# A sandwich of two feed-forward blocks around windowed attention: scores computed once and probabilities transposed by DMA

## The chip, the cores and the metric

The kernel runs on one core of a Trainium2 chip. The metric is the time of one execution on the device in microseconds (us). The time of the kernel before is the median of three runs; its profile is of one further execution. TensorE (PE), VectorE (DVE), ScalarE (ACT), GpSimd (POOL) and the queue of SyncE (SP) each take their instructions in the order written and wait for one another by semaphores.

## The reference

The input x is 8 sequences of 512 tokens with 512 features. Three residual blocks follow each other:

```
x = x + 0.5 * ffn(layernorm(x), w_gate_up, w_proj)      # "A"
x = x + attention(layernorm(x), Wq, Wk, Wv, Wo)         # "B"
x = x + 0.5 * ffn(layernorm(x), w_gate_up, w_proj)      # "C"
```

`ffn` quantises both weights to bfloat16 ternary values (per group of 64 elements: scale = mean of the magnitudes, q = round(w/scale) clipped to -1..1, weight = q*scale), computes h = silu(gate)*up with 2048 hidden features, normalises h by its root mean square and projects back. `attention` has 32 heads of 16 features; a query sees itself and the 128 keys before it, so a block of 128 queries needs the keys of its own block and of the block before (of its own alone, if it is the first of its sequence): softmax(q k^T / 4) v, then Wo.

## The kernel before, in words

The 4096 tokens are 32 blocks of 128. A prologue quantises the feed-forward weights in 12 units of 128x2048 (`UNITS`), transposes them on TensorE and keeps them in SBUF. Per unit ScalarE takes magnitudes and signs (`parts`), VectorE sums groups (`scales`) and compares, adds and multiplies (`quantise`); GpSimd forms 'scale minus magnitude' (`differ`) and multiplies by the sign in five of the units (`give_sign`), with an all-reduce of the maxima after the eighth. Between units the first block's gate and up products run. VectorE then takes the largest magnitude of each attention weight (`largest`), GpSimd reduces it over the partitions, and the attention weights are scaled and split in steps 2 to 10.

Then comes a software pipeline. Every engine and the SP queue walk through `range(STEPS)`, and each step runs the pieces whose offset fits: `block_at(step, offset)` is the block b with step = offset + 8b, `group_at(step, offset)` is the pair (block, group) for pieces that run once per step. So a new block enters every 8 steps, and each of its stages has an offset (`UP_A`, `Q_AT`, `SCORES`, `PV`, `UP_C`, ...). A's feed-forward chunks of block b run in steps 8b to 8b+3, C's in steps 8b+36 to 8b+39. From step 36 to step 251 every step therefore holds one feed-forward chunk of 512 hidden features, of A (step mod 8 = 0 to 3) or of C (4 to 7), and one group of 4 heads of some block in each attention stage. Before and after these steps only part of them holds a chunk. STEPS is 8*31 + 42 = 290. In a step:

- TensorE: `scores` (four matmuls 128x256, queries in the partitions), the gate product, the up product, `scores_t` (eight matmuls 128x128, keys in the partitions), `down` of the chunk of the step before, `prob_v`, and in steps mod 8 = 0, 1, 3, 7 a projection of 12 matmuls 128x512 (Q, K, V, Wo).
- VectorE: square means, `masked_max` (row maxima of the group, with the mask added), low halves of q, k, v, of the layer norms' splits, residual additions, `normalise_o` in even steps, the low half of o, then `gated`, `hidden`, the low half of the probabilities, the low half of the hidden values (`h_lo`), and last the layer norms' statistics and `xhat`.
- ScalarE: high halves of q, k, v, xh and oh, `tanh_half` (of the gate product), the high half of the probabilities, two Relu that scale `scores_t` into `prob`, `h_hi`, the square, and one Exp over 128x1024 (or half of that in a sequence's first block).
- GpSimd: small powers, the sum of the squares, and two `affine_select` that mask `prob`.
- SP: one transposing DMA for each of q, k, xh (A, B, C) and oh in a block, plus one more of q after `max_rows` has written the negative row maxima of the whole block into spare rows of q. The transposed scores thus arrive with the maximum subtracted, which is why they start a block later (`SCORES_T` = 20) than `scores` (12).

Keys come in two halves of 128 (the block before and the block itself); in the first block of a sequence only the second exists, and the operands of the scores, maxima and probabilities are half as wide. Values of 32 bits are carried as a high and a low half of 16 bits.

The transposed scores stand in a ring of three banks, `ps_s` (`score_bank`). Two waits of the kernel before on ScalarE matter for the order of a step: the tanh waits for the gate product alone, and `oh` in steps mod 8 = 6 waits for the last normalisation of its block:

```
    s, b, c = ffn_at(step)
    if s and not (s == "A" and b == 0):
        tanh_half(s, b, c, step)
    ...
    act.wait_ge(p_st, 16 * b + 2 * g + o + 1)
```

## Time and profile before

| | |
|---|---|
| median of 3 runs | 2278.78 us (2277.72 to 2279.49) |
| profiled execution | 2278.95 us, of which the span of instructions is 2277.2 us |
| mean granted TensorE clock | 0.961 of 2.4 GHz |
| busy over the span: PE | 2063.2 us (91%) |
| DVE | 1784.5 us (78%) |
| ACT | 1401.9 us (62%) |
| POOL | 768.5 us (34%) |
| DMA queue of SP | 117.47 MB, 25.7% of 16 engines' span |

Busy time is an average over a prologue of about 150 us, a ramp, a steady part and a drain. A start time in the timeline, counted from the span's start, dates a step; the difference of two starts on one engine is what an instruction takes there, waits included, while a mean duration also holds latency in which the next instruction may already run. The idle time ahead of a group of instructions is listed with the engine and the instruction that ended it.

### The profile page before, as it was taken

The numbers are of one execution on the slowest core, as the hardware profiler recorded it, in microseconds if no ns is written. First come the engines' busy times: TensorE is split into PE (matmuls) and PEld (weight loads), VectorE is DVE, ScalarE is ACT, GpSimd is POOL, SyncE is SP. The second block draws the span as 40 slices with busy tenths as digits, with TensorE's granted clock in tenths as the row PEclk, the third lists the DMA queues.
The fourth block names the chain that finished last, engine by engine and source line by source line (L and its number), as shares of the span: only waits on it lengthen the run. The fifth ranks groups of instructions, "written<-read, shape, count | busy, mean of one in ns | idle before, by whom it ended". The sixth has DMA issues, their size and how long they took to land. (4 is left out here: it accounts for less than half of the span.)

```text
span 2277.2 us, 64890 instructions
## 1 busy us (share of the span) xinstructions
PE 2063.2 (91%) x26752; PEld 1496.5 (66%) x26752; DVE 1784.5 (78%) x4393; ACT 1401.9 (62%) x2073; POOL 768.5 (34%) x963
## 2 busy tenths in 40 slices
PE   1327789999999999999999999999999999999877
PEld 1315557777777777777777767777777777776556
DVE  8965678787887788877887878878878888887764
ACT  5523357665676566765767566765666566666672
POOL 4431123332333333333333333333333233333332
PEclk9668889999999999999999999999999999999989
DMA  4221222222332222222322222332223222223210
GB/s 161 74 83 29 52 47 53 53 48 57 57 50 44 46 48 57 57 53 48 57 58 54 39 46 49 57 57 52 48 57 57 57 36 46 49 52 48 43 34 20
DMA packets 351269, 121.62 MB, mean 53 GB/s; under 512 B 336128, under 2 KB 336128, under 8 KB 350464
## 3 DMA queue, kind: packets, MB, share of 16 engines
q1 hardware_dynamic: 350976, 117.47, 25.7%
q8 instruction: 213, 3.49, 0.6%
q14 instruction: 80, 0.66, 0.1%
HBM read 25.17 MB, written 8.39 MB: 15 GB/s over the span
## 5 line engine op out<-in xcount | busy, mean ns | idle before, releaser
L778 DVE CUSTOM_DVE_ANT_0 masked<-ps_s,mask 128x256 f32<-128x256 f32 (+1 forms) x1024 | 338.4, 386 | 199.3 <-PE ps_s L983 199.1
L622 ACT ACTIVATE prob<-ps_s,neg_exp_scale 128x512 f32<-128x512 f32 (+1 forms) x512 | 295.9, 629 | 123.2 <-PE ps_s L997 123.2
L504 POOL TENSOR_TENSOR acc_A<-acc_A,sq 128x512 f32<-128x512 f32 x96 | 125.7, 1310 | 568.2 <-ACT sq L639 568.0
L536 ACT ACTIVATE hid<-ps_g 128x512 f32<-128x512 f32 x256 | 151.8, 593 | 259.9 <-PE ps_g L950 259.8
L752 DVE TENSOR_TENSOR pt<-prob,pt 128x1024 f16<-128x1024 f32 (+1 forms) x256 | 276.8, 1081 | 6.9 <-ACT pt L614 6.9
L1007 PE MATMUL ps_y<-wp_t,h_hi 128*128 128x512 bf16 x1024 | 267.2, 384 | 14.9 <-ACT h_hi L532 14.9
L504 POOL TENSOR_TENSOR acc_C<-acc_C,sq 128x512 f32<-128x512 f32 x96 | 134.0, 1395 | 434.8 <-ACT sq L639 434.8
L645 ACT ACTIVATE prob<-prob,prob_bias 128x1024 f32<-128x1024 f32 (+1 forms) x256 | 265.0, 1035 | 0.6
L1007 PE MATMUL ps_y<-wp_t,h_lo 128*128 128x512 bf16 x1024 | 264.6, 381 | 0.0
L950 PE MATMUL ps_g<-xt_C,wgu_t 128*128 128x128 f16 x4096 | 255.0, 221 | 7.4 <-DMA xt_C<-xh 6.8
L950 PE MATMUL ps_g<-xt_A,wgu_t 128*128 128x128 f16 x4096 | 260.5, 224 | 1.3 <-DMA xt_A<-xh 1.3
L614 ACT ACTIVATE pt<-prob 128x1024 f16<-128x1024 f32 (+1 forms) x256 | 241.5, 943 | 24.8 <-POOL prob L514 24.8
L950 PEld LDWEIGHTS ps_g<-xt_A,wgu_t 128*128 128x128 bf16 x4096 | 239.1, 100 | 23.9 <-issue 18.7
L950 PEld LDWEIGHTS ps_g<-xt_C,wgu_t 128*128 128x128 bf16 x4096 | 233.6, 99 | 29.8 <-issue 18.5
L767 DVE SCALAR_TENSOR_TENSOR hid<-ps_u,h_scale_u,hid 128x512 f32<-128x512 f32 x252 | 189.2, 751 | 80.7 <-PE ps_u L950 51.8
L950 PE MATMUL ps_u<-xt_A,wgu_t 128*128 128x128 f16 x4096 | 250.6, 219 | 0.0
L950 PE MATMUL ps_u<-xt_C,wgu_t 128*128 128x128 f16 x4096 | 249.6, 219 | 0.0
L950 PEld LDWEIGHTS ps_u<-xt_A,wgu_t 128*128 128x128 bf16 x4096 | 235.3, 98 | 0.0
L512 POOL TENSOR_SCALAR_AFFINE_SELECT prob<-prob 128x512 f32<-128x512 f32 x192 | 130.0, 677 | 310.3 <-ACT prob L645 310.3
L950 PEld LDWEIGHTS ps_u<-xt_C,wgu_t 128*128 128x128 bf16 x4096 | 234.1, 98 | 0.0
L752 DVE TENSOR_TENSOR h_lo<-hid,h_hi 128x512 f16<-128x512 f32 x256 | 176.4, 689 | 46.0 <-ACT h_hi L532 44.1
L532 ACT ACTIVATE h_hi<-hid 128x512 f16<-128x512 f32 x256 | 161.1, 629 | 70.7 <-DVE hid L767 52.5
(152 smaller groups left out, 3311.3 us busy)
## 6 DMA issues: line engine op xcount, KB each, us to landing
stream<-in_L_attn_x_dram SPq DMA_DIRECT2D x32, 256.0 KB, 3.7
out_dram<-stream SPq DMA_DIRECT2D x32, 256.0 KB, 2.5
stream<-in_L_ffn_w_gate_up_dram SPq DMA_DIRECT2D x4, 1024.0 KB, 5.2
prob<-in_L_ffn_w_gate_up_dram SPq DMA_DIRECT2D x4, 1024.0 KB, 5.6
stream<-in_L_ffn_w_proj_dram SPq DMA_DIRECT2D x2, 1024.0 KB, 4.9
prob<-in_L_ffn_w_proj_dram SPq DMA_DIRECT2D x2, 1024.0 KB, 4.8
stream<-in_L_attn_Wq_dram SPq DMA_DIRECT2D x1, 1024.0 KB, 5.4
prob<-in_L_attn_Wk_dram SPq DMA_DIRECT2D x1, 1024.0 KB, 7.6
```

The costliest lines, as they stand in the source:

```text
L504: pool.tensor_tensor(out=acc[s][:, :], in0=acc[s][:, :], in1=sq[:, step % 2, :], op=ALU.add).then_inc(g_acc[s], 1)
L512: pool.affine_select(out=p4[:, :, 0, :], in_=p4[:, :, 0, :], compare_op=ALU.is_ge, fill=0.0, base=0, pattern=[[0, 4], [-1, P]], channel_mu ...
L532: act.activation(dst, src, ACT.Copy, scale=scale).then_inc(done, 1)
L536: act.activation(hid[:, step % 2, :], ps_g[:, :], ACT.Tanh, scale=0.5 * 2.0 ** -XS_LOG2).then_inc(a_tanh[s], 1)
L614: act.activation(halves(pt[:, 0, g % 2, :, :], b), halves(prob[:, g % 2, :, :], b), ACT.Copy).then_inc(a_ph, 1)
L622: act.activation(halves(prob[:, g % 2, 4 * o:4 * o + 4, :], b), halves(score_bank(step, 2 + o).rearrange("p (t q) -> p t q", q=P), b), ACT ...
L645: act.activation(p, p, ACT.Exp, bias=prob_bias[:, 0:1], scale=-1.0).then_inc(a_exp, 1)
L752: dve.tensor_tensor(out=dst, in0=src, in1=hi, op=ALU.subtract).then_inc(done, 1)
L767: dve.scalar_tensor_tensor(out=dst, in0=ps_u[:, :], scalar=scale, in1=hid[:, step % 2, :], op0=ALU.mult, op1=ALU.mult).then_inc(d_h[s], 1)
L778: m = dve.tensor_tensor_reduce(masked[:, g % 2, 2 * pair + o, first:2 * P], score_bank(step, o)[:, pair * 2 * P + first:(pair + 1) * 2 * P ...
L950: t = pe.matmul(bank[:, j * P:(j + 1) * P], wgu_t[:, k, at:at + P], xt[s][:, part, k, :], start=(k == 0 and part == 0), stop=(k == KD - 1 ...
L1007: t = pe.matmul(ps_y[:, :], part[:, (step - 1) % 3, j * P:(j + 1) * P], wp_t[:, 4 * c + j, :], start=(c == 0 and j == 0 and part is h_hi), ...
```

## The change

Scores are computed once, with the queries in the partitions, and the probabilities are formed there. The masked scores that `masked_max` writes stay in `masked`. ScalarE turns the group's four row maxima into biases (an Identity operation of 128x4) and runs four Exp in place, one for each head, in the step of the scores and ahead of the tanh. One step later ScalarE writes the high half and VectorE the low half of the probabilities, now ahead of the other work of the step, and SP transposes both halves with one DMA into `pt`; `prob_v` follows in the step after. `scores_t`, its two Relu, the 128x1024 Exp, `max_rows`, its transpose of q and GpSimd's masks go. All attention stages behind the scores and the whole of C move 8 steps forward, so that a block passes through 34 steps instead of 42 (STEPS = 282). The ring of score banks becomes two fixed banks, and the sums of squares get a bank of their own (`ps_q`).

In the prologue ScalarE widens the group scales to 128x2048 (`spread`, into the space of k4), VectorE subtracts the magnitudes itself and multiplies by the sign in all 12 units, and ScalarE's order becomes signs, store, magnitudes of the next unit, spread. The maxima of the attention weights move into steps 0 and 1, behind the hidden values. The number that stands for a masked key is -2^100 for -3e38.

```diff
-    M_AT = SCORES + 7
-    SCORES_T = 20
-    PROB = SCORES_T + 1
-    PV = SCORES_T + 2
+    PROB = SCORES + 1
+    PV = SCORES + 2
     NORM = PV + 1
-    SPLIT_O, WO_AT = NORM + 7, 31
-    LN_C, XHAT_C, SPLIT_C = 32, 33, 34
-    UP_C, SQ_C, ADD_C = 36, 40, 41
+    SPLIT_O, WO_AT = NORM + 7, 23
+    LN_C, XHAT_C, SPLIT_C = 24, 25, 26
+    UP_C, SQ_C, ADD_C = 28, 32, 33
...
@@ SyncE @@
-                b = block_at(step, M_AT)
-                if b is not None:
-                    sp.wait_ge(d_m, b + 1)
-                    sp.wait_ge(p_s, 16 * b + 16)
-                    transpose(qt[:, b % QRING, :, :], q4[:, b % 2, :, :, :].rearrange("p a b c -> p (a b c)"), t_qm)
+                b, g = group_at(step, PROB)
+                if b is not None:
+                    sp.wait_ge(d_pl, 8 * b + g + 1)
+                    need(sp, p_pv, 8 * b + g - 1)
+                    first = first_half(b)
+                    transpose(pt[:, g % 2, first:2, :, :, :].rearrange("p a b c d -> p (a b c) d"),
+                              prob[:, g % 2, first:2, :, :, :].rearrange("p a b c d -> p (a b c d)"), t_p[g % 2])
...
@@ GpSimd @@
-            for n in range(NTU):
-                differ(n)
-                if n % 2 == 0 and n > 0:
-                    give_sign(n - 1)
...
-                b, g = group_at(step, SCORES_T)
-                if b is not None:
-                    p4 = prob[:, g % 2, :, :].rearrange("p (j h) q -> p j h q", h=2)
-                    pool.wait_ge(a_exp, 8 * b + g + 1)
-...
@@ ScalarE, prologue @@
+            def spread(n):
+                act.wait_ge(w_grp, n + 1)
+                need(act, w_dif, n)
+                act.activation(w_wide.rearrange("p (g k) -> p g k", g=G64),
+                               grp_scale[:, n % 2, :].unsqueeze(2).to_broadcast([P, G64, 64]),
+                               ACT.Copy).then_inc(w_spread, 1)
...
@@ ScalarE, in a step, behind the copies of q, k, v @@
+                b, g = group_at(step, PROB)
+                if b is not None:
+                    act.wait_ge(a_exp, 8 * b + g + 1)
+                    need(act, t_p[g % 2], 16 * (4 * b + g // 2))
+                    act.activation(prob_part(prob[:, g % 2, :, 0, :, :], b), prob_f32(b, g), ACT.Copy).then_inc(a_ph, 1)
@@ ScalarE, in a step, behind xh and oh @@
+                b, g = group_at(step, SCORES)
+                if b is not None:
+                    act.wait_ge(d_mx, 16 * b + 2 * g + 2)
+                    need(act, a_exp, 8 * (b - 1) + g + 1)
+                    act.activation(exp_bias[:, 4 * g:4 * g + 4], row_max[:, 4 * g:4 * g + 4], ACT.Identity,
+                                   bias=prob_bias[:, 0:1], scale=neg_exp_scale[:, 0:1]).then_inc(a_bias, 1)
+                    act.wait_ge(a_bias, 8 * b + g + 1)
+                    for h in range(4):
+                        p = masked[:, g % 2, h, P * first_half(b):2 * P]
+                        t = act.activation(p, p, ACT.Exp, bias=exp_bias[:, 4 * g + h:4 * g + h + 1],
+                                           scale=exp_scale[:, 0:1])
+                    t.then_inc(a_exp, 1)
+
                 s, b, c = ffn_at(step)
                 if s and not (s == "A" and b == 0):
                     tanh_half(s, b, c, step)
...
@@ VectorE, quantise @@
+                dve.wait_ge(w_spread, n + 1)
+                need(dve, w_q[n % 2], n // 2)
+                dve.tensor_tensor(out=diff, in0=w_wide, in1=w, op=ALU.subtract).then_inc(w_dif, 1)
...
@@ VectorE, in a step, behind the low half of v @@
+                b, g = group_at(step, PROB)
+                if b is not None:
+                    take_lo(prob_part(prob[:, g % 2, :, 1, :, :], b), prob_f32(b, g),
+                            prob_part(prob[:, g % 2, :, 0, :, :], b), a_ph, 8 * b + g + 1, d_pl)
...
@@ TensorE @@
-                b, g = group_at(step, SCORES_T)
-                if b is not None:
-                    need(pe, a_neg, 2 * groups_by(step - 1, SCORES_T))
-                    need(pe, d_mx, 2 * groups_by(step, SCORES) - (group_at(step, SCORES)[0] is not None))
-                    if g == 0:
-                        pe.wait_ge(t_qm, 16 * (b + 1))
-                    scores_t(b, g, step)
...
                 b, g = group_at(step, PV)
                 if b is not None:
-                    pe.wait_ge(d_pl, 8 * b + g + 1)
+                    pe.wait_ge(t_p[g % 2], 16 * (4 * b + g // 2 + 1))
```

## Rows read from the trace of the kernel before

**Rows 1.** Stretches of time: length, then busy us (instructions) of each engine, clock, DMA.
```profile
800.00:1600.00 800.00, 791.10 (x10464) 572.15 (x10461) 648.26 (x1695) 523.12 (x800) 277.83 (x367) 1.00 0.28 52
...
2105.00:2132.00 27.00, 19.98 (x188) 9.98 (x189) 18.41 (x63) 16.39 (x20) 8.37 (x14) 0.81 0.43 79
```
**Rows 2.** Timeline of TensorE in two steps: start, us, operation.
```profile
1355.86 0.39 PE L983 MATMUL ps_s<-kt,qt 48*128 48x256 f16 x4
...
1365.02 0.39 PE L983 MATMUL ps_s<-kt,qt 48*128 48x256 f16 x4
...
1369.02 0.40 PE L997 MATMUL ps_s<-qt,kt 64*128 64x128 f16 x8
...
1371.57 0.39 PE L983 MATMUL ps_s<-kt,qt 48*128 48x256 f16 x4
```
**Rows 3.** Timeline of ScalarE: the tanh of steps 24, 36 and 252.
```profile
285.87 0.60 ACT L536 ACTIVATE hid<-ps_g 128x512 f32<-128x512 f32 x1 [2.93 <-PE ps_g L950]
...
371.51 0.60 ACT L536 ACTIVATE hid<-ps_g 128x512 f32<-128x512 f32 x1 [1.56 <-PE ps_g L950]
...
2077.61 0.60 ACT L536 ACTIVATE hid<-ps_g 128x512 f32<-128x512 f32 x1 [1.56 <-PE ps_g L950]
```
**Rows 4.** Groups of ScalarE by shape, 800 to 1600 us: busy us, mean ns | idle before.
```profile
L645 ACT ACTIVATE prob<-prob,prob_bias 128x1024 f32<-128x1024 f32 x76 | 86.9, 1143 | 0.0
L614 ACT ACTIVATE pt<-prob 128x1024 f16<-128x1024 f32 x75 | 78.8, 1050 | 1.3 <-POOL prob L514 1.3
...
L645 ACT ACTIVATE prob<-prob,prob_bias 128x512 f32<-128x512 f32 x26 | 18.5, 710 | 0.0
```
**Rows 5.** Timeline of all engines in the drain, where the feed-forward chain runs almost alone.
```profile
2229.41 0.68 DVE L761 SCALAR_TENSOR_TENSOR hid<-hid,ps_g 128x512 f32<-128x512 f32 x1
...
2230.29 0.75 DVE L767 SCALAR_TENSOR_TENSOR hid<-ps_u,h_scale_u,hid 128x512 f32<-128x512 f32 x1 [0.20 <-PE ps_u L950]
...
2231.13 0.63 ACT L532 ACTIVATE h_hi<-hid 128x512 f16<-128x512 f32 x1 [1.88 <-DVE hid L767]
...
2231.80 0.69 DVE L752 TENSOR_TENSOR h_lo<-hid,h_hi 128x512 f16<-128x512 f32 x1 [0.76 <-ACT h_hi L532]
...
2233.65 0.60 ACT L536 ACTIVATE hid<-ps_g 128x512 f32<-128x512 f32 x1 [1.37 <-PE ps_g L950]
```
**Rows 6.** Timeline of VectorE in the steady part.
```profile
1228.05 0.69 DVE L738 BATCH_NORM_STATS2 st_C<-stream 128x6 f32<-128x512 f32 x1
...
1229.06 0.21 DVE L809 TENSOR_SCALAR sq_mean_C<-ps_o,rms_eps 128x1 f32<-128x1 f32 x1
...
1236.71 0.69 DVE L752 TENSOR_TENSOR h_lo<-hid,h_hi 128x512 f16<-128x512 f32 x1 [0.22 <-ACT h_hi L532]
1237.32 1.50 DVE L747 TENSOR_SCALAR xhat<-stream,mean_var_C,rstd_C 128x512 f32<-128x512 f32 x1
...
1242.07 0.42 DVE L798 TENSOR_REDUCE o_sum<-ps_o 128x128 f32<-128x256 f32 x1
...
1242.90 0.68 DVE L761 SCALAR_TENSOR_TENSOR hid<-hid,ps_g 128x512 f32<-128x512 f32 x1
...
1255.63 0.42 DVE L778 CUSTOM_DVE_ANT_0 masked<-ps_s,mask 128x256 f32<-128x256 f32 x1 [1.71 <-PE ps_s L983]
...
1257.01 0.08 DVE L778 DVE_READ_ACCUMULATOR2_ANT row_max<- 128x1 f32 x1
```
**Rows 7.** Groups of VectorE in the prologue, 0 to 178 us.
```profile
L674 DVE TENSOR_TENSOR kt<-kt,q 128x2048 bf16<-128x2048 bf16 x12 | 41.8, 3480 | 6.9 <-POOL q L448 6.9
...
L676 DVE TENSOR_TENSOR q<-kt,q 128x2048 bf16<-128x2048 bf16 x12 | 21.3, 1773 | 0.4
...
L661 DVE TENSOR_SCALAR grp_scale<-grp_sum 128x32 bf16<-128x32 f32 x12 | 11.1, 921 | 0.4
...
L683 DVE TENSOR_TENSOR pt<-q,qt 128x2048 bf16<-128x2048 bf16 x7 | 8.6, 1225 | 0.2
```
**Rows 8.** DMA issues: times, median us from issue to landing.
```profile
qt<-q SPq DMA_TRANSPOSE x64, 4.4
```

More of the change, by code:

```diff
@@ L48, in macaron @@
     V_LOG2 = 19
-    M_LOG2 = 15
     RING = 8
@@ L639, in step_of @@
                     act.activation(squares, hid[:, step % 2, :], ACT.Square).then_inc(a_sq[s], 1)
-                b, g = group_at(step, SCORES_T)
-                if b is not None:
-                    act.wait_ge(a_neg, 16 * b + 2 * g + 2)
-                    p = halves(prob[:, g % 2, :, :], b)
-                    act.activation(p, p, ACT.Exp, bias=prob_bias[:, 0:1], scale=-1.0).then_inc(a_exp, 1)
             for step in range(STEPS):
@@ L768, in hidden, with masked_max @@
                                          op0=ALU.mult, op1=ALU.mult).then_inc(d_h[s], 1)
[L770 to L772 removed]
+            def masked_max(b, g):
+                need(dve, d_pl, 8 * b + g - 1)
+                need(dve, a_bias, 8 * (b - 1) + g + 1)
                 first = 0 if b % BPS else P
@@ L905, in step_of @@
                         hidden(s, bf, c, hid[:, step % 2, :], step, h_scale_u[:, 0:1])
-                b, g = group_at(step, PROB)
-                if b is not None:
-                    take_lo(halves(pt[:, 1, g % 2, :, :], b), halves(prob[:, g % 2, :, :], b),
-                            halves(pt[:, 0, g % 2, :, :], b), a_ph, 8 * b + g + 1, d_pl)
+                if step in (0, 1):
+                    for m in ((Q, K), (V, O))[step]:
+                        largest(m)
                 if s:
@@ L975, in project, with scores @@
                 t.then_inc(done, 1)
-            def scores(b, g, step):
+            def scores(b, g):
                 place = b % BPS
@@ L982, in scores @@
                         rows = slice(64 * o, 64 * o + 3 * DK)
-                        t = pe.matmul(score_bank(step, o)[:, pair * 2 * P + (0 if place else P):(pair + 1) * 2 * P],
+                        at = o * CH + pair * 2 * P
+                        t = pe.matmul(ps_s[:, at + P * first_half(b):at + 2 * P],
                                       qt[rows, b % QRING, 2 * g + pair, :],
@@ L988, in scores @@
                             t.then_inc(p_s, 1)
-            def scores_t(b, g, step):
-                place = b % BPS
-                for pair in range(2):
-                    for half in ((0, 1) if place else (1,)):
-                        for o in range(2):
-                            at = pair * 2 * P + half * P
-                            rows = slice(64 * o, 64 * o + 64)
-                            t = pe.matmul(score_bank(step, 2 + o)[:, at:at + P],
-                                          kt[rows, 2 * g + pair, place - 1 + half, :],
-                                          qt[rows, b % QRING, 2 * g + pair, :], start=True, stop=True)
-                            if pair and half:
-                                t.then_inc(p_st, 1)
             def down(s, b, c, step):
@@ L1018, in prob_v @@
                         for n, (half, part) in enumerate(products):
-                            t = pe.matmul(ps_o[:, at:at + VW], pt[:, part, g % 2, (o * 2 + pair) * 2 + half, :],
+                            t = pe.matmul(ps_o[:, at:at + VW], pt[:, g % 2, half, part, 2 * pair + o, :],
                                           v[:, place - 1 + half, hd, 0:VW], start=(n == 0), stop=(n == len(products) - 1))
@@ L1051, in step_of @@
                     need(pe, d_mx, 2 * groups_by(step - 1, SCORES))
-                    need(pe, a_neg, 2 * groups_by(step - 1, SCORES_T) - 1)
                     if g == 0:
@@ L1055, in step_of @@
                         pe.wait_ge(t_k, 16 * (b + 1))
-                    scores(b, g, step)
+                    scores(b, g)
                 s, b, c = ffn_at(step)
@@ L1104, in step_of @@
                         need(pe, d_on, 4 * b + g // 2)
-                    for sq_s, offset in (("A", SQ_A), ("C", SQ_C)):
-                        bs = block_at(step - 1, offset)
-                        if bs is not None:
-                            pe.wait_ge(d_sqm[sq_s], bs + 1)
                     prob_v(b, g)
```

155 lines of the change are left out of this document (58 added, 97 removed).

## The prediction

> **What bounds the kernel now.** I read the stretches first. Between 800 and 1600 us TensorE is busy for 791 of 800 us at full clock, VectorE for 648, ScalarE for 523 and GpSimd for 278, and the DMA engines for 0.28 of the time [rows 1]. So in the steady part TensorE sets the pace, but VectorE is only a fifth behind it. Then TensorE's timeline: a step without a projection lasts 6.55 us (scores at 1365.02, the next scores at 1371.57), one with a projection 9.16 us (1355.86 to 1365.02), and the transposed scores span 0.40 us of each [rows 2]. Four of the eight steps of a block carry a projection (step mod 8 = 0, 1, 3, 7). Then ScalarE's tanh of the first chunk of a phase, which dates the steps: step 24 at 285.87, step 36 (where C's FFN starts) at 371.51, step 252 at 2077.61 [rows 3]. So 216 full steps, 27 blocks, take 1706.1 us: 63.2 us a block.
>
> **What leaves TensorE.** The transposed scores go: about 0.33 us a step once the overlap of the last matmul is taken off the 0.40 [rows 2], 2.6 us a block. TensorE's own work was 0.989 of 63.2 us [rows 1], 62.5 us, and falls to 59.9. Call it 60.8 with the short gaps between steps. By that alone the change would be a clear gain.
>
> **What is added to the chain between VectorE and ScalarE.** Here I chose another reading than "the busiest engine". Before, the tanh of step s waited only for TensorE. Now ScalarE's order in a step is: bias, four Exp, then tanh. The bias waits for the row maxima of the same step, and on VectorE these stand behind h_lo of step s-1. h_lo needs h_hi, that needs hidden, that needs gated, and that needs tanh of s-1. So there is a loop of exactly one step that TensorE takes no part in. Its links, from rows:
> The four masked maxima: 1.38 us to the last read, 0.08 for it, 1.46 (1255.63 to 1257.01) [rows 6]. Handing over to ScalarE 0.10, as from hidden to h_hi below. The bias operation (128x4): ScalarE's 128x512 and 128x1024 exponentials differ by 433 ns, 0.85 ns an element; the 1024 copy without a pointer takes 93 ns less than the exponential with one (1050 against 1143) [rows 4]. So the fixed part without a pointer is about 0.2 us, with two pointers (scale and bias) 0.385, and 0.03 for the wait on itself. Bounds: 0.2 and 0.5. The new Exp (128x256, two pointers): 710 less 216 is 494, plus 93 is 587 ns; starts follow each other about 0.10 us closer than durations, so 0.485, and four are 1.94 us. Bounds: 1.58 if the second pointer is free, 2.35 if nothing overlaps. Tanh 0.60 (2233.65) and 0.03 to gated, as from the end of h_hi to h_lo. From gated to hidden 0.88 (2229.41 to 2230.29), to h_hi 0.84, to h_lo 0.67 [rows 5]. To the next operation of VectorE 0.61 (1236.71 to 1237.32) [rows 6], and 0.1 for the wait for the scores. Sum: 7.65 us for every step, against 6.2 us of TensorE's work in a step without a projection and 8.8 in one with it.
>
> What stands in the loop beside that depends on the step. Between the maxima and gated VectorE has about 3.1 us for other work (the low half of the probabilities, the same operation as before, somewhat over a microsecond; a normalisation 0.83, 1242.07 to 1242.90 [rows 6]; one or two operations of 0.6 to 0.7), which covers it. Behind h_lo there is no cover. Statistics cost 1.0 (1228.05 to 1229.06) in steps 0, 3 and 5; xhat of A 0.5 in step 4; xhat of B and C 1.4 in steps 6 and 1, since their row shows 1.50 us at the moment GpSimd adds the squares (1237.32) [rows 6], which the change leaves there. In step 6 ScalarE's copy of o_norm waits for maxima, probabilities, split and normalisation in turn and stands ahead of the bias: 3.0 us more, where before it stood ahead of a tanh that did not wait for maxima. The eight steps from step 0: 8.75, 8.95, 7.65, 8.6, 8.1, 8.6, 12.0, 7.65, together 70.4 us. TensorE would need 60.8, and its projections fall in steps where the loop has caught up, so they add nothing. In the first block of a sequence (one in four) the operands are half as wide: by the same slopes the maxima take 0.93 and the exponentials 1.50 (estimates), so 6.7 for a step; there TensorE's projection steps lead again in steps 1 and 3, and I work out 63.7. With 21 blocks of the one and 7 of the other a block costs 68.7 us, 5.5 more than now.
>
> Beside the sum stands a rule of the Trainium skill, "VectorE: DVE Perf Modes", section "The TRN2 errata": operations that read SBUF pay a fixed latency per instruction, many small tiles pay it each time, and ScalarE's is given as 224 cycles plus one per element. That speaks against four 256-wide exponentials in place of a 1024-wide one. An estimate by that page is 0.40 us for each, 1.6 for four, 0.34 less per step than my rows give; the total would be about 2320 us. No row shows a 256-wide exponential.
>
> **The transposes.** Eight transposes of the probabilities are added per block and the one of the row maxima goes. One of this size lands in 4.4 us [rows 8]. The DMA share of 0.28 [rows 1] is 17.7 us a block for three of the 512 KB size, four of half the size and two plain 256 KB ones. With 0.7 us for a plain one, a large one fills all engines for 3.2 us. After: ten large ones, 39 us of 68.7. The low half is ready 2.5 to 3.1 us behind the start of the maxima, the product with v comes some 13 us behind them, so there are about 5 us to spare even behind another transpose. On SP the new one stands ahead of those of xt_B, xt_C, xt_A and ot; each of these has a step or more. I take nothing for it. If that cover went, SP's next waits would hold xt and with it the gate product.
>
> **GpSimd's masks and the max rows** leave engines that don't bind: nothing. With them the wait for rms_inv goes too.
>
> **The weights phase.** VectorE sets it. The comparison takes 3.48 us in the mean where GpSimd runs, with 6.9 us of waiting besides; the addition 1.77; the scale 0.92 against a quiet 0.18, an estimate from its smallest neighbours; a product without a neighbour 1.225 [rows 7]. Without GpSimd: (3.48-1.22)x12 + (1.77-1.22)x12 + (0.92-0.2)x12 + 6.9 = 49 us less. Added on VectorE: 12 subtractions and 5 products of 1.25, 21 us. Net 28 us. ScalarE's widened copy (1.8 us by the same width) fits: its unit is some 7.3 us against VectorE's 8.8. The maxima of the attention weights now lie between other work, some 4 us more. Together 32 us; bounds 20 and 36.
>
> **Fewer steps.** Full steps go from 216 to 224, 28 blocks. To the first full step: the eight steps that go are the 85.6 us from step 24 to 36 less four full steps (31.6), 54 [rows 3]. So 371.5, less 32, less 54, plus 5 for the loop in the early attention steps: 291. Behind the last full step before lie 38 steps in 2277.2-2077.6 = 199.6 us, 5.25 each; 30 remain, 158, and 10 for the loop: 168. Sum: 291 + 28 x 68.7 + 168 = 2383 us of span. The profiled execution was 1.75 us longer than its span (2278.95) and agrees with the median, 2278.78, within 0.2. So **2385 us**, 4.7% slower. The same line gives the break-even: 64.9 us a block.
>
> **The rivals.**
> *TensorE stays the bound* (the other side). If bias, exponentials and tail were shorter, so that a step of the loop averaged under 7.6 us and not 8.6, each block would cost 60.8: 291 + 1702 + 168 + 2 = 2163 us. For it: ScalarE and VectorE both have idle time. Against: the order of the instructions, in which that idle time is waiting. It beats the old time once a block is under 64.9. Chance 0.08.
> *The second pointer and the short operations cost nothing*: 0.54 less a step, mid blocks 66.1, first ones 62.3, so 65.2 a block and 2286 us. Chance 0.05, 0.03 of it within the bound of no change, 0.02 below.
> *TensorE's clock falls.* It now idles some 8 us a block. Where it was busy for 20 of 27 us the granted clock was 0.81 [rows 1], a mix of 1.2 and 2.4 GHz. At that clock its 60.8 us become 75 and bind: 2561 us. Against: it stays near 0.9 busy. Chance 0.09, most of it for a part of this price.
> *The transposes bind.* If ten large ones took 6.1 and four small ones 4 us one after another, a block would be 78 us and the time 2645. Chance 0.04.
>
> **Range.** From 2300 (block 65.7: the low bounds of Exp and bias with the xhat stalls kept) to 2420 (block 70.0 or a few us more in the ends: no overlap of the Exps). It leaves out TensorE's case, most of the clock's and the transposes'. Within 0.2% is about what a measurement of this kernel can tell from no change. Slower 0.74+0.09+0.04 = 0.87, same 0.03, faster 0.08+0.02 = 0.10.
>
> **What would show it.** Right: in the steady part TensorE falls to about 0.88 busy and waits ahead of the gate product for VectorE's gated; ScalarE's first Exp or bias waits for row_max; the step mod 8 = 6 is the longest at 12 us; the product with v never waits for DMA; steady blocks of 68 to 70 us with a short one in four; weights done 30 us earlier. Wrong: if TensorE still runs at 0.98, if the Exps overlap more than 0.10 us, if xhat no longer takes 1.50, or if waits for pt appear.

## The result and the profile after

The changed kernel takes 2438.66 us (median of four runs, 2437.78 to 2438.86) against 2278.25 before (2277.25 to 2279.49): ratio 1.070 [1.0685, 1.0722]. The forecast was 2385 us with a range of 2300 to 2420. The direction was right, and so was the loop that was to set the pace; the time lies 54 us above the forecast and 19 above the range. The profiled execution has a span of 2436.8 us and a mean granted clock of 0.928 (0.961 before).

The stretches first, the same 800 us as in [rows 1]:

```profile
800.00:1600.00 800.00, 713.01 (x8816) 526.94 (x8813) 586.72 (x1504) 493.02 (x899) 156.28 (x171) 0.95 0.51 92
```

All four engines are less busy than before, TensorE at 0.89 for 0.99: none of them is the bound by its sum. The DMA share has gone from 0.28 to 0.51. Then the waits of the same stretch (who waited for whom: us in total, times, longest):

```profile
ACT h_hi L504 <- DVE hid L754: 159.7, 90, 2.1
DVE hid L748 <- ACT hid L508: 98.1, 89, 2.2
...
ACT exp_bias L602 <- DVE row_max L765: 54.8, 56, 2.1
...
ACT oh L504 <- DVE o_norm L780: 44.9, 12, 4.2
PE ps_g L924 <- DVE hid L748: 40.1, 12, 3.6
...
PE ps_y L969 <- DVE stream L792: 26.3, 20, 2.4
PE ps_o L981 <- DVE o_norm L780: 20.6, 21, 1.8
```

ScalarE and VectorE wait for each other in turn, which is what a loop through both looks like, and TensorE waits for what VectorE hands it. No wait of TensorE for a transposed `pt` is among them. One turn of the loop stands in the timeline of a step mod 8 = 3 (start, us, operation):

```profile
1201.45 0.42 DVE L765 CUSTOM_DVE_ANT_0 masked<-ps_s,mask 128x256 f32<-128x256 f32 x1
...
1202.95 0.39 ACT L602 ACTIVATE exp_bias<-row_max,prob_bias,neg_exp_scale 128x4 f32<-128x4 f32 x1 [0.67 <-DVE row_max L765]
...
1203.37 2.07 ACT L607 ACTIVATE masked<-masked,exp_bias,exp_scale 128x256 f32<-128x256 f32 x4
...
1205.35 0.57 ACT L508 ACTIVATE hid<-ps_g 128x512 f32<-128x512 f32 x1
...
1205.96 0.69 DVE L748 SCALAR_TENSOR_TENSOR hid<-hid,ps_g 128x512 f32<-128x512 f32 x1 [1.91 <-ACT hid L508]
...
1206.86 0.75 DVE L754 SCALAR_TENSOR_TENSOR hid<-ps_u,h_scale_u,hid 128x512 f32<-128x512 f32 x1 [0.21 <-DVE hid L748]
...
1207.70 0.63 ACT L504 ACTIVATE h_hi<-hid 128x512 f16<-128x512 f32 x1 [1.78 <-DVE hid L754]
...
1208.37 0.69 DVE L739 TENSOR_TENSOR h_lo<-hid,h_hi 128x512 f16<-128x512 f32 x1 [0.76 <-ACT h_hi L504]
...
1208.97 0.69 DVE L725 BATCH_NORM_STATS2 st_A<-stream 128x6 f32<-128x512 f32 x1
...
1210.06 0.42 DVE L765 CUSTOM_DVE_ANT_0 masked<-ps_s,mask 128x256 f32<-128x256 f32 x1
```

From the first maximum to the first operation behind h_lo it is 7.52 us (1201.45 to 1208.97), then 1.09 of statistics, and the next step begins. The forecast's sum was 7.65, of which 0.1 was for a wait for the scores that does not occur here. The new operations came out as sized, by shape in 800 to 1600 us:

```profile
L607 ACT ACTIVATE masked<-masked,exp_bias,exp_scale 128x256 f32<-128x256 f32 x280 | 145.2, 589 | 2.3
...
L602 ACT ACTIVATE exp_bias<-row_max,prob_bias,neg_exp_scale 128x4 f32<-128x4 f32 x91 | 35.1, 385 | 54.9 <-DVE row_max L765 54.8
```

An Exp takes 589 ns (587 forecast, from the slopes of [rows 4]), the bias 385 (385). Four Exp span 2.07 us, and tanh starts 1.98 behind the first (1.94 forecast).

By the tanh of steps 28 and 252 (303.15 and 2260.80) the span divides into 303.2 + 28 x 69.92 + 176.0. The forecast was 291 + 28 x 68.7 + 168. So 34 us of the miss lie in the steady part, 12 in the ramp, 8 in the drain.

### The profile page after: what moved, and what is told of

Same layout as the page of the kernel before. It is cut to its first block and busy times, and to the rows that moved or that the text cites. A ratio compares the mean times of both kernels' runs of the same rounds, so it can differ in the third digit from the quotient of the medians.

```text
span 2436.8 us, 61174 instructions
## 1 busy us (share of the span) xinstructions
PE 2049.2 (84%) x24960; PEld 1513.8 (62%) x24960; DVE 1761.1 (72%) x4347; ACT 1482.2 (61%) x2597; POOL 439.2 (18%) x497
## 5 line engine op out<-in xcount | busy, mean ns | idle before, releaser
L607 ACT ACTIVATE masked<-masked,exp_bias,exp_scale 128x256 f32<-128x256 f32 (+1 forms) x1024 | 503.7, 562 | 8.6
L924 PE MATMUL ps_g<-xt_C,wgu_t 128*128 128x128 f16 x4096 | 303.0, 243 | 108.3 <-DVE hid L748 101.3
L748 DVE SCALAR_TENSOR_TENSOR hid<-hid,ps_g 128x512 f32<-128x512 f32 x256 | 176.0, 688 | 277.5 <-ACT hid L508 277.0
L924 PEld LDWEIGHTS ps_g<-xt_C,wgu_t 128*128 128x128 bf16 x4096 | 278.5, 110 | 134.5 <-DVE hid L748 115.1
L739 DVE TENSOR_TENSOR prob<-masked,prob 128x1024 f16<-128x1024 f32 (+1 forms) x256 | 283.2, 1106 | 5.4 <-ACT prob L586 5.4
L924 PE MATMUL ps_u<-xt_C,wgu_t 128*128 128x128 f16 x4096 | 280.6, 233 | 0.0
L924 PEld LDWEIGHTS ps_u<-xt_C,wgu_t 128*128 128x128 bf16 x4096 | 266.7, 106 | 0.0
L586 ACT ACTIVATE prob<-masked 128x1024 f16<-128x1024 f32 (+1 forms) x256 | 240.0, 937 | 0.4
L981 PEld LDWEIGHTS ps_o<-v,pt 128*128 128x128 f16 x3584 | 122.9, 96 | 167.3 <-issue 103.1
L981 PE MATMUL ps_o<-v,pt 128*128 128x33 f16 x3584 | 129.9, 178 | 93.9 <-DVE o_norm L780 76.1
```

Of the source, the lines that this page charges most:

```text
L586: act.activation(prob_part(prob[:, g % 2, :, 0, :, :], b), prob_f32(b, g), ACT.Copy).then_inc(a_ph, 1)
L607: t = act.activation(p, p, ACT.Exp, bias=exp_bias[:, 4 * g + h:4 * g + h + 1], scale=exp_scale[:, 0:1])
L739: dve.tensor_tensor(out=dst, in0=src, in1=hi, op=ALU.subtract).then_inc(done, 1)
L748: dve.scalar_tensor_tensor(out=hid[:, step % 2, :], in0=hid[:, step % 2, :], scalar=1.0, in1=ps_g[:, :], op0=ALU.add, op1=ALU.mult).then_i ...
L924: t = pe.matmul(bank[:, j * P:(j + 1) * P], wgu_t[:, k, at:at + P], xt[s][:, part, k, :], start=(k == 0 and part == 0), stop=(k == KD - 1 ...
L981: t = pe.matmul(ps_o[:, at:at + VW], pt[:, g % 2, half, part, 2 * pair + o, :], v[:, place - 1 + half, hd, 0:VW], start=(n == 0), stop=(n ...
```

## The experiments

All are edits of the changed kernel unless they say "the kernel before". "A block" is a quarter of the time between ScalarE's copies of q of blocks 13 and 17, which holds one first block of a sequence and three others; it is 63.2 us before and 70.0 us after.

| run | us | ratio to before | a block |
|---|---|---|---|
| after | 2438.7 | 1.070 | 70.0 |
| e1 tanh first | 2217.3 | 0.973 | 62.4 |
| e2 Exp last | 2412.1 | 1.059 | 68.9 |
| e3 one Exp | 2312.0 | 1.015 | 65.8 |
| e4 before, new weights phase | 2249.2 | 0.987 | 63.2 |
| e5 oh late | 2321.5 | 1.019 | 65.8 |
| e6 half transposes | 2434.8 | 1.069 | 70.0 |
| e7 tanh first, oh late | 2202.3 | 0.967 | 61.9 |
| e8 = e7, additions early | 2165.2 | 0.950 | 60.7 |
| e9 norms early | 2346.8 | 1.030 | 66.9 |
| e10 an extra operation | 2520.5 | 1.106 | 72.6 |
| e11 before, the same extra | 2300.5 | 1.010 | 63.8 |
| e12 = e8, norms early | 2165.0 | 0.950 | 61.5 |
| e13 short projections | 2375.4 | 1.043 | 68.1 |

The intervals of the ratios are 0.0014 to 0.0019 to either side.

### e1: the tanh ahead of bias and Exp

```diff
@@ ScalarE, in a step @@
+                s, b, c = ffn_at(step)
+                if s and not (s == "A" and b == 0):
+                    tanh_half(s, b, c, step)
                 b, g = group_at(step, SCORES)
                 if b is not None:
...
-                s, b, c = ffn_at(step)
-                if s and not (s == "A" and b == 0):
-                    tanh_half(s, b, c, step)
```

> The changed kernel with ScalarE's tanh issued ahead of the bias and the four Exp of the same step, nothing else. Theory (the loop maxima - bias - Exp - tanh - gated - hidden - h_hi - h_lo sets the step): tanh, gated and hidden leave the loop, what is left of it is 1.46 + 0.10 + 0.42 + 1.94 + 0.67 + 0.71 = 5.3 us, below TensorE's 6.2, so TensorE sets most steps again; only the step mod 8 = 6, where the copy of o_norm waits for VectorE, stays at some 10 us. A block of 63 to 65 us for 69.9, 2250 to 2290 us in all. Rival one (the transposes through DMA or the waits of the product with v and of ps_y bind): the time stays within 10 us of 2438. Rival two (VectorE's and ScalarE's work itself, not its order, is too much): 2400 us or more.

2217.3 us, ratio 0.973 [0.9713, 0.9746]: 221 us from one moved instruction, and more than was expected. It leaves no room for either rival: the same transposes, the same work on each engine, another order. ScalarE in a step mod 8 = 4 of this kernel:

```profile
1235.56 0.60 ACT L508 ACTIVATE hid<-ps_g 128x512 f32<-128x512 f32 x1 [1.04 <-PE ps_g L924]
1236.05 0.38 ACT L606 ACTIVATE exp_bias<-row_max,prob_bias,neg_exp_scale 128x4 f32<-128x4 f32 x1
1236.46 2.07 ACT L611 ACTIVATE masked<-masked,exp_bias,exp_scale 128x256 f32<-128x256 f32 x4
1238.95 0.63 ACT L504 ACTIVATE h_hi<-hid 128x512 f16<-128x512 f32 x1 [0.42 <-DVE hid L754]
```

Between tanh and h_hi ScalarE has to wait for gated and hidden in any case. The bias and the four Exp now fill that gap, and 0.42 us of waiting is left of the 1.78 in the changed kernel. The tanh waits for TensorE again.

### e2: bias and Exp at the end of ScalarE's step

```diff
@@ ScalarE, in a step: the block of bias and Exp moved @@
                     act.activation(squares, hid[:, step % 2, :], ACT.Square).then_inc(a_sq[s], 1)
+                b, g = group_at(step, SCORES)
+                if b is not None:
+                    act.wait_ge(d_mx, 16 * b + 2 * g + 2)
...
```

> The changed kernel with bias and Exp moved to the end of ScalarE's step, behind h_hi and the square. Theory of the loop: nothing of the FFN chain waits for the maxima of its own step any more; what is left is the maxima to Exp to the high half of the probabilities of the next step, with slack. TensorE binds at 60.8 us a block but for step 6: 61 to 63.5 us a block, 2190 to 2255 us. If TensorE's clock falls or the transposes bind instead, 2330 us or more, because the probabilities now come later; waits of TensorE for pt would show.

2412.1 us: the time is 157 us above the expected range, and its reason fails with it. It falls among the times of the rival (2330 or more), but not for the rival's reasons: between 800 and 1600 us TensorE never waits for pt, and its mean clock is 0.96 for 0.95. ScalarE from one h_hi to the next:

```profile
1195.33 0.63 ACT L504 ACTIVATE h_hi<-hid 128x512 f16<-128x512 f32 x1 [2.43 <-DVE hid L754]
1195.87 0.61 ACT L615 ACTIVATE sq<-hid 128x512 f32<-128x512 f32 x1
1196.39 0.37 ACT L621 ACTIVATE exp_bias<-row_max,prob_bias,neg_exp_scale 128x4 f32<-128x4 f32 x1
1196.79 2.08 ACT L626 ACTIVATE masked<-masked,exp_bias,exp_scale 128x256 f32<-128x256 f32 x4
...
1199.25 1.04 ACT L586 ACTIVATE prob<-masked 128x1024 f16<-128x1024 f32 x1
1200.20 0.58 ACT L508 ACTIVATE hid<-ps_g 128x512 f32<-128x512 f32 x1
1204.04 0.63 ACT L504 ACTIVATE h_hi<-hid 128x512 f16<-128x512 f32 x1 [3.26 <-DVE hid L754]
```

VectorE in the same turn:

```profile
1200.33 1.23 DVE L739 TENSOR_TENSOR prob<-masked,prob 128x1024 f16<-128x1024 f32 x1 [0.25 <-ACT prob L586]
...
1202.30 0.68 DVE L748 SCALAR_TENSOR_TENSOR hid<-hid,ps_g 128x512 f32<-128x512 f32 x1
```

Nothing waits for the maxima here, and still a step takes 8.7 us (1195.33 to 1204.04). Steps are cyclic: behind h_hi of one step is ahead of the tanh of the next, so the Exp still stand between h_hi and tanh. The edit also adds a wait that the changed kernel does not have. The high half of the probabilities now comes right behind the Exp that feed it, and VectorE's low half, which stands ahead of gated, waits for it: 69.0 us in 66 waits between 800 and 1600 us, none in the changed kernel. Gated starts at 1202.30, 1.5 us behind the end of the tanh, and ScalarE idles 3.26 us until hidden. The 27 us of gain are the sum of both effects, so e2 does not price the chain through the maxima alone.

That two chains run side by side in the changed kernel, VectorE's through the maxima and ScalarE's own of square, high half, bias, Exp and tanh, is seen in its own trace. In the turn of 7.52 us shown above the bias waited 0.67 us for the maxima, so ScalarE's own sequence would have taken some 6.9 (an estimate from these two numbers). Between 800 and 1600 us 56 of the 91 bias operations waited for a maximum, 35 did not. e1 takes the Exp out of both chains.

### e3: one Exp for four

```diff
-                    for h in range(4):
-                        p = masked[:, g % 2, h, P * first_half(b):2 * P]
-                        t = act.activation(p, p, ACT.Exp, bias=exp_bias[:, 4 * g + h:4 * g + h + 1],
-                                           scale=exp_scale[:, 0:1])
+                    p = masked[:, g % 2, :, P * first_half(b):2 * P]
+                    t = act.activation(p, p, ACT.Exp, bias=prob_bias[:, 0:1], scale=tiny[:, 0:1])
```

> The changed kernel, but the group's Exp is one instruction over 128x1024 with a constant bias and a constant small scale, both by pointer, so every probability is about the same number: the maxima are taken and the bias operation is issued but not used. Order and all waits as in the changed kernel. It sizes the term of the four Exp. Theory of the loop: 1.94 us becomes about 1.05, 0.9 us less in every step that the loop sets, some 6 us a block and 165 to 185 us in all with the ramp: 2255 to 2275 us. Rival (DMA or TensorE waits bind): under 30 us less.

2312.0 us, 127 us less; 165 to 185 were expected. The row of the new Exp, against four that span 2.07 us:

```profile
L608 ACT ACTIVATE masked<-masked,prob_bias,tiny 128x1024 f32<-128x1024 f32 x74 | 91.8, 1241 | 2.5
```

It saves 0.83 us a step, 6.6 a block if every step were set by the loop; 4.2 came back. In a middle block the steps mod 8 = 3, 5 and 6 are 0.84 us shorter, steps 2 and 4 by 0.44 and 0.57, and steps 0 and 1 keep their 8.94 and 9.31 us: something else sets them (e13).

### e4: the new weights phase in the kernel before

The edits of the prologue alone (`spread`, `magnitudes`, `signs`, `quantise`, the maxima in steps 0 and 1) in the kernel before; its steps stay.

> The kernel before with the new weights phase alone (widened scales from ScalarE, VectorE subtracts and signs, the maxima of the attention weights in steps 0 and 1); its steps are untouched. Theory: VectorE's units fall from some 11 us to 8.7, and the whole is 30 us earlier, 2248 us. If the gain is lost in the ramp (attention weights, which come in fixed steps), 2260 us or more.

2249.2 us, 29 us less, ratio 0.987 [0.9859, 0.9888]. The forecast had 32 (28 of it for the units, bounds 20 and 36). Q of the first block is copied 28.9 us earlier than before and the block is the same 63.2, so the gain reaches the end whole. The rows of VectorE in the changed kernel's first 150 us show how well a clean neighbour's duration carries over [rows 7]:

```profile
L662 DVE TENSOR_TENSOR q<-kt,q 128x2048 bf16<-128x2048 bf16 x12 | 14.7, 1225 | 0.4
L660 DVE TENSOR_TENSOR kt<-kt,q 128x2048 bf16<-128x2048 bf16 x12 | 14.7, 1225 | 0.4
```

### e5: the copy of o_norm behind the tanh

```diff
@@ ScalarE: behind tanh_half instead of ahead of bias and Exp @@
+                b = block_at(step, SPLIT_O)
+                if b is not None:
+                    need(act, t_o, 16 * b)
+                    copy(oh[:, 0, :], o_norm[:, :], d_on, 4 * b + 4, a_oh)
@@ VectorE: the low half behind hidden instead of ahead of gated @@
+                b = block_at(step, SPLIT_O)
+                if b is not None:
+                    take_lo(oh[:, 1, :], o_norm[:, :], oh[:, 0, :], a_oh, b + 1, d_ol)
```

> The changed kernel with one piece moved: in the step mod 8 = 6 ScalarE's copy of o_norm comes behind the tanh and not ahead of the bias and the Exp, and VectorE's low half of o behind hidden. Theory of the loop: the 12.1 us step falls to about 8, 4 us a block; TensorE then idles less ahead of step 7, its clock there stays up, and it is less late for the scores of steps 7 to 2, up to 1 us more. 65 to 66 us a block for 69.9, 2300 to 2335 us. If TensorE's clock drop in step 7 were what counts by itself, the gain would be 6 us a block, under 2275 us; if something else holds step 6, under 30 us of gain.

2321.5 us, 117 us less, within the range of the loop theory. The changed kernel's long step, mod 8 = 6, in its timeline:

```profile
1230.90 0.63 ACT L504 ACTIVATE oh<-o_norm 128x512 f16<-128x512 f32 x1 [3.88 <-DVE o_norm L780]
...
1235.18 3.60 PE L924 MATMUL ps_g<-xt_C,wgu_t 128*128 128x128 f16 x32 [3.35 <-DVE hid L748]
...
1238.87 0.41 DVE L765 CUSTOM_DVE_ANT_0 masked<-ps_s,mask 128x256 f32<-128x256 f32 x1
```

The step lasts 12.10 us (from 1226.77), 12.0 forecast, and 8.96 in e5. TensorE idles 3.35 us behind it, and then the gate product takes 3.60 us for the usual 1.96. The stretches show why (the clock is the third figure from the right):

```profile
1235.20:1238.20 3.00, 3.00 (x29) 3.00 (x30) 2.12 (x3) 2.03 (x3) 0.81 (x1) 0.50 0.19 36
...
1242.00:1246.00 4.00, 4.00 (x35) 1.96 (x32) 1.74 (x4) 2.23 (x5) 0.00 (x0) 1.00 0.92 175
```

At 0.50, the lower of the two levels (1.2 of 2.4 GHz), TensorE loses 1.6 us there and another 1.1 in the up product (3.07 us for 1.95), and is late into the next steps. In e5 the mean clock between 800 and 1600 us is 0.99 for 0.95, and the steps mod 8 = 7 and 0 are 0.48 and 0.28 us shorter. So of 4.2 us a block 3.1 are the long step itself and under one comes from the steps behind it.

### e6: half of the transposed bytes

```diff
-                    first = first_half(b)
+                    first = 1
                     transpose(pt[:, g % 2, first:2, :, :, :].rearrange("p a b c d -> p (a b c) d"),
```

> The changed kernel, but each DMA of the probabilities transposes only the keys of the block itself (256 KB for 512 KB); in place of the other half the product with v reads ones. Order and waits stay. Theory (transposes are hidden): under 10 us from 2438. If they cost time, through the product with v, the queue of SP or the DMA engines: 30 us or more faster.

2434.8 us, 4 less, and the same 70.0 a block, while the DMA share between 800 and 1600 us falls from 0.51 to 0.37: in the steady part of the changed kernel the transposes are free.

### e7 and e8: the order that beats both kernels

e7 joins the edits of e1 and e5, but its copy of o_norm stands ahead of bias and Exp (in e5 it stands behind them). e8 moves three pieces of VectorE as well:

```diff
@@ VectorE, in a step: ahead of the low half of the probabilities @@
+                b = block_at(step, ADD_A)
+                if b is not None:
+                    add_ffn("A", b, d_x1)
+                b = block_at(step, ADD_C)
+                if b is not None:
+                    add_ffn("C", b, d_x3)
+                b, g = group_at(step, NORM)
+                if b is not None and g % 2:
+                    normalise_o(b, g // 2)
                 b, g = group_at(step, PROB)
                 if b is not None:
                     take_lo(prob_part(prob[:, g % 2, :, 1, :, :], b), prob_f32(b, g),
```

> Tanh ahead of bias and Exp (as in the first run) and the copy of o_norm behind both tanh and ahead of the bias, the low half of o behind hidden. There TensorE idles some 3 us a block, and the step mod 8 = 6 still lasts 11.2 us. Theory: about 1.5 us a block comes back, 2165 to 2195 us. If TensorE binds fully already: no change from 2217.

> As the run before, and on VectorE the two residual additions of the FFN and the normalisation of o are moved ahead of the low half of the probabilities. TensorE's waits for ps_y (18 us in 800) and ps_o (8 in 800) should go, which is 2 us a block at the most; the probabilities come 0.8 us later in half of the steps, hidden. 2130 to 2185 us, at least 10 us below the run before. Rival: the low half comes too late for the next scores' buffers or for the transposes, and TensorE's waits move to pt: no gain.

e7: 2202.3 us, 15 less than e1; 22 to 52 were expected. e8: 2165.2 us, ratio 0.950 [0.9488, 0.9516], 37 less again. TensorE's waits ahead of its products into ps_y and ps_o, which the forecast had not named, are 18.3 and 7.8 us between 800 and 1600 us in e1, still 13.9 and 14.9 in e7, and gone in e8. Its steady part:

```profile
800.00:1600.00 800.00, 781.88 (x10182) 575.09 (x10179) 668.80 (x1743) 572.58 (x1042) 166.09 (x197) 1.00 0.61 106
```

TensorE is 0.98 busy at full clock, with 60.7 us a block. That is the 60.8 the forecast had for a TensorE-bound block, and 2165 us is the 2163 of its first rival. So the change, with another order on two engines, is 5% faster than the kernel before; 1.3% of it is the weights phase (e4). A small wait for a transpose does appear in this faster kernel: TensorE waits 5.9 us in these 800 for ot. What the early additions would give the kernel before was not tested; its TensorE was busy for 791 of 800 us already [rows 1].

### e9: statistics and xhat ahead of gated

The pieces `LN_B` to `XHAT_A` of VectorE's step move from behind h_lo to the place before `gated`.

> The changed kernel with one piece of VectorE's step moved: the statistics and the xhat of the layer norms stand ahead of gated, where the prediction says that 3.1 us lie free, and not behind h_lo, where it says that there is no cover. Theory of the prediction (the loop runs through the maxima): of the 6.3 us a block that stood behind h_lo 3 to 5 go: 65 to 67 us a block, 2290 to 2350 us. Rival (ScalarE's own sequence h_hi, square, high half of the probabilities, bias, Exp, tanh is nearly as long, and the maxima are mostly in time): under 1.5 us a block, 2395 us or more.

2346.8 us, 3.1 us a block less, within the range expected by the forecast's theory and far from its rival. Part of it has another source. Between 800 and 1600 us, the changed kernel and then e9:

```profile
L734 DVE TENSOR_SCALAR xhat<-stream,mean_var_B,rstd_B 128x512 f32<-128x512 f32 x12 | 18.1, 1506 | 0.0
L734 DVE TENSOR_SCALAR xhat<-stream,mean_var_C,rstd_C 128x512 f32<-128x512 f32 x11 | 16.6, 1505 | 0.0
```

```profile
L734 DVE TENSOR_SCALAR xhat<-stream,mean_var_B,rstd_B 128x512 f32<-128x512 f32 x12 | 6.5, 541 | 0.0
L734 DVE TENSOR_SCALAR xhat<-stream,mean_var_C,rstd_C 128x512 f32<-128x512 f32 x12 | 6.5, 539 | 0.0
```

The same instruction takes 0.54 us once it no longer starts as GpSimd adds the squares. Two of them make up to 1.9 us a block. e9 does not separate that from the place in the loop. The step mod 8 = 1 keeps its 9.31 us even without the long xhat.

### e10 and e11: an operation that nobody reads

```diff
+                if s:
+                    dve.tensor_reduce(extra[:, :], mask[:, :].unsqueeze(1).to_broadcast([P, 2, 2 * P]), AX.X, ALU.max)
                 b = block_at(step, LN_B)
```

> The changed kernel with an operation added on VectorE behind h_lo in every step with a chunk: a maximum over a constant, 128x512, about 0.6 us, that nobody reads. Theory of the prediction: all of it enters the loop in the steps that the maxima set, 4 to 4.7 us a block, 2550 to 2575 us. Rival (ScalarE's own sequence): it is absorbed for the most part, under 2480 us.

> The same added operation in the kernel before. TensorE binds there and VectorE idles some 12 us of 63 a block: 2278 to 2295 us. If VectorE's chain is close behind TensorE there too, 2310 us or more.

The row of the changed kernel's variant, 680 ns, about 0.6 from start to start:

```profile
L892 DVE TENSOR_REDUCE extra<-mask 128x2 f32<-128x512 f32 x87 | 59.1, 679 | 0.0
```

e10 costs 82 us, between the two expectations. By steps mod 8 = 0 to 7 of a middle block the lengths went from 8.94, 9.31, 8.00, 8.61, 8.11, 8.60, 12.10, 7.98 to 9.24, 9.30, 8.60, 9.21, 8.71, 9.19, 12.11, 8.11. In steps 2 to 5 the whole 0.6 arrives: VectorE's chain through h_lo and the maxima sets these steps alone. In steps 1 and 6 nothing arrives, and that is no proof of slack: there the xhat of C and of B stands behind the added operation, starts 0.6 us further into GpSimd's addition and takes 0.916 us for 1.505 (all 22 of them between 800 and 1600 us), which gives the 0.6 back. The forecast of e10 had not seen this. Steps 0 and 7 take up part of it. In the kernel before the same operation costs 22 us, a little above the range expected: TensorE's bound absorbs most of it.

### e12: e9's edit on e8

> The eighth run (tanh ahead, o late, additions early; 2165 us) with the statistics and xhat ahead of gated. TensorE binds at 60.7 us a block there, so the steady part has nothing to give: 2150 to 2175 us. If gated comes later than TensorE can bear, 2180 us or more.

2165.0 us, the same as e8 within 0.2. Where TensorE is the bound, what the loop loses is worth nothing. (The block reads 61.5 because one of its four took 3 us more; the next four average 60.8.)

### e13: projections of 4 matmuls

```diff
-                    for n, (part, w) in enumerate(((0, wat_hi), (0, wat_lo), (1, wat_hi))):
-                        t = pe.matmul(ps_m[:, :], tokens[:, part, k, :], w[m][:, k, :], start=(k == 0 and n == 0),
-                                      stop=(k == KD - 1 and n == 2))
+                    t = pe.matmul(ps_m[:, :], tokens[:, 0, k, :], wat_hi[m][:, k, :], start=(k == 0),
+                                  stop=(k == KD - 1))
```

> The changed kernel, but each projection (Q, K, V, Wo) keeps the product of the two high halves alone, 4 matmuls for 12; the other two products are left out, so q, k, v and the output lack their low parts. It tests the step 'the projections fall in steps where the loop has caught up, so add nothing'. A step was 8.94, 9.31, 8.00 and 7.98 us long at step mod 8 = 0, 1, 2, 7 where the prediction had 8.75, 8.95, 7.65 and 7.65; step 1 stayed at 9.30 in four other variants. Theory now (in these four steps the projection and ScalarE's copy of it enter the loop, and in the ramp and the drain, where TensorE runs at the low clock, a projection of 5 us does): 0.7 to 1.3 us a block and 5 to 20 us in the ends, 2385 to 2415 us. If the prediction's step holds and the excess is from elsewhere: 2428 us or more.

2375.4 us, 63 less, more than was expected, and nowhere near "hidden". In middle blocks the steps mod 8 = 0, 1, 2 and 7 now last 8.65, 8.94 to 9.20, 7.55 or 8.00, and 7.50 us, for 8.75, 8.95, 7.65 and 7.65 in the prediction: without two thirds of each projection they come close to what the loop alone was to give. VectorE's waits for the scores ahead of the maxima fall from 12.2 us (33 times) between 800 and 1600 us to 0.2 (once), and ScalarE's waits for the projections of q are gone. The clock is no rival here, since its mean between 800 and 1600 us is 0.94, no higher than before the edit (0.95). The block loses 1.8 us, the ramp up to step 28 10.5, the drain 5. The changed kernel's own timeline shows the place, the turn from step 1 to step 2:

```profile
1192.57 0.38 PE L947 MATMUL ps_m<-wk_hi,xt_B 128*128 128x512 f16 x1
...
1192.88 0.39 PE L958 MATMUL ps_s<-kt,qt 48*128 48x256 f16 x4
...
1193.05 1.02 ACT L504 ACTIVATE k<-ps_m 128x1024 f16<-128x1024 f32 x1 [1.51 <-PE ps_m L947]
...
1193.45 0.42 DVE L765 CUSTOM_DVE_ANT_0 masked<-ps_s,mask 128x256 f32<-128x256 f32 x1 [0.28 <-PE ps_s L958]
...
1193.97 1.05 ACT L586 ACTIVATE prob<-masked 128x1024 f16<-128x1024 f32 x1
...
1194.92 0.62 ACT L504 ACTIVATE xh<-xhat 128x512 f16<-128x512 f32 x1
...
1195.44 0.38 ACT L602 ACTIVATE exp_bias<-row_max,prob_bias,neg_exp_scale 128x4 f32<-128x4 f32 x1
```

The scores stand behind K's projection, so the maxima wait for them. And ScalarE's copy of k waits 1.51 us for the projection and stands ahead of the high half, the split and the bias, which comes 0.5 us behind the last maximum with no wait for it. Both chains get later by TensorE.

## Why the prediction was right or wrong

**The loop** was right, link by link: 7.52 us measured for 7.65. Steps mod 8 = 3 to 6 are 8.61, 8.11, 8.60, 12.10 for 8.6, 8.1, 8.6, 12.0. e1 shows that the place of the tanh is the cause, e3, e5 and e10 that single links count at nearly full price in the steps that the loop sets. (The eight steps of the forecast add up to 70.3, not 70.4; that is 2 us in all.)

**Why it is a loop** was half of it. "The bias waits for the row maxima" holds for 56 of 91 steps, but ScalarE's own sequence from h_hi through Exp to tanh is nearly as long, some 6.9 us for 7.52 (e2).

**The step that failed** is "its projections fall in steps where the loop has caught up, so they add nothing". They cost at least 1.8 us a block, which is what two thirds of their matmuls gave back (e13). Steps 7, 0, 1 and 2 were 7.98, 8.94, 9.31 and 8.00 for 7.65, 8.75, 8.95 and 7.65, together 1.2 us, nearly all of the excess of such a block and 34 us over the 28 blocks. "A loop of exactly one step that TensorE takes no part in" is wrong in these steps: scores come behind a projection, and ScalarE copies its result ahead of the bias. In steps 7 and 0 the low clock behind step 6's idle stretch is needed for it too, since e5, which keeps the projections and shortens that stretch, has 7.50 and 8.66 there; in steps 1 and 2 e5 keeps 9.30 and 8.00. The rival "TensorE's clock falls" came true for the gate and up products of one step in eight, not for the whole.

**The ends** were under-sized by 20 us, and they are what took the time out of the range. The forecast gave 5 us for the loop in the early steps and 10 behind the last full step. Dated by the tanh, steps 11 to 16 (190.76 to 214.67) now take 23.9 us for 19.5, steps 19 to 24 (236.44 to 269.43) 33.0 for 24.6. The loop explains only the first of these, and in part: with the tanh first (e1) they take 22.2 and 33.1, in e8 21.5 and 33.2. From step 8 to step 28 e1 is 4.0 us faster than the changed kernel, so the 5 us for the loop were about right. What the sum left out is another thing. It took the steps up to 24 as they stood, while attention stages that came later before now fall into them. The stretch from step 19 to step 24, before and after:

```profile
261.23:285.87 24.64, 15.62 (x150) 9.76 (x148) 17.53 (x63) 11.41 (x21) 6.59 (x10) 0.79 0.26 54
```

```profile
236.44:269.43 32.99, 18.92 (x181) 10.09 (x179) 23.55 (x72) 20.85 (x38) 4.07 (x6) 0.74 0.52 96
```

TensorE, VectorE and ScalarE have 3.3, 6.0 and 9.4 us more to do there. That the 8.4 us follow from this work is argued, since no run takes these stages out again. The changed kernel's timeline in these steps reads:

```profile
246.93 0.36 PE L981 MATMUL ps_o<-v,pt 128*128 128x33 f16 x8 [1.22 <-DMA pt<-prob]
...
257.31 0.64 PE L981 MATMUL ps_o<-v,pt 128*128 128x33 f16 x16 [1.68 <-DMA pt<-prob]
...
259.94 0.61 PE L947 MATMUL ps_m<-wo_hi,ot 128*128 128x512 f16 x1 [2.00 <-DMA ot<-oh]
...
265.53 0.42 DVE L765 CUSTOM_DVE_ANT_0 masked<-ps_s,mask 128x256 f32<-128x256 f32 x1 [5.19 <-PE ps_s L958]
```

Transposes are not covered in these short steps, and Wo's projection, at a granted clock of 0.53, takes 5 us with the next scores behind it. "The product with v never waits for DMA" is right in the steady part (e6) and wrong here; what it costs is small, since half the bytes gave 4 us back. The projections cost more: e13 took 3.0 us out of steps 19 to 24. Of the 10.5 us that it took out of the whole ramp 3.4 lie in steps 8 to 11, which last 21.1 us in the changed kernel and 21.3 in the kernel before, so they are no part of the excess.

Behind step 252 the changed kernel takes 176.0 us, e1 168.6 and e8 164.3. The order is thus worth 7 to 12 us there, for 10 in the forecast, and its 158 for 30 steps without the loop was at least 6 short.

**The weights phase** gained 29 to 30 us for 32: e4, and the tanh of step 8 comes at 169.66 us for 199.79.

**TensorE's saving** was right: 60.7 us a block where it binds (e8) for 60.8. Identity among Exp and tanh brought no table loads: the whole trace has one, at 0.73 us, like that of the kernel before (0.80).

**The page's figure.** "VectorE: DVE Perf Modes", section "The TRN2 errata", of the Trainium skill gave, by the estimate ahead, 0.40 us for an Exp and a total of 2320; the row shows 0.589, and the measurement decides. That many small tiles pay a fixed part each time does hold: one Exp over 128x1024 takes 1.24 us where four span 2.07, and e3 is 127 us faster by it.

**The range** was too narrow because the term that the text called hidden, and the work that moves into the ramp, had no bound of their own. With the ends as forecast a block of 69.92 us gives 2419 us, 1 us inside the range. That this upper end nearly covered the projections was luck: it had been set for another reason, Exps that do not overlap.

## What to carry to other kernels

In engines that take instructions in order, look for the gap that a chain already leaves (here between tanh and h_hi, where ScalarE waits for VectorE), and put new work there; the same work one place earlier cost 221 us. Moving it "to the end of the step" is no cure when steps repeat, since the end of one is the front of the next. Whatever is called hidden in a sum needs a price for the case that it is not, above all an engine that idles behind the new bound, because its late results and its low clock come back at other places.

## What the runs showed of the hardware

- xhat (128x512) takes 1.505 us where it starts with GpSimd's addition, 0.916 where it starts 0.6 us later (e10) and 0.54 where the two do not meet (e9); the 128x2048 comparison took 3.48 us beside GpSimd [rows 7] and 1.225 without it.
- In the step mod 8 = 6, 3.35 us of idling of TensorE was followed by a gate and an up product of 3.60 and 3.07 us for 1.96, at a granted clock of 0.50 to 0.59, and then full clock again.
- A 128x1024 Exp with bias and scale by pointer takes 1241 ns, against 1143 with one pointer [rows 4] and 4 x 589 in four pieces, which span 2.07 us.
